# Storing the convolution's result tiles from GpSimd's queue instead of SyncE's

## The reference

```python
# layer 0: x and the weight are quantised to whole numbers of -127..127 by their largest magnitude
qx, sx = _quantize_per_tensor(_gn(x));  qw, sw = _quantize_per_tensor(weight)
out = conv3x3(qx, qw, padding=1) * (sx * sw / 127**2) + bias
x = x + out
# layer 1: a Fourier layer that keeps 32 x 16 frequencies
xf = rfft2(_gn(x));  y = einsum('ijab,ejab->eiab', R, xf[:, :, ix, :16])
x = x + irfft2(zeros.at[:, :, ix, :16].set(y))
```

## Time and profile before

| | us |
|---|---|
| median of 3 runs | 3955.18 |
| lowest and highest | 3941.83, 3962.70 |
| profiled execution, its own time | 3964.72 |
| its span, first to last instruction | 3962.8 |
| PE busy in the span | 2813.2 (71%) |
| DVE busy | 3387.9 (85%) |
| ACT busy | 2548.8 (64%) |
| POOL busy | 6.0 (0%), 16 instructions |

### The profile page before, as it was taken

How to read it: one execution, slowest core, us unless ns; L and a number is a source line. 1 busy time by engine, 2 the same in 40 slices (tenths; PEclk the granted TensorE clock), 3 DMA queues, 4 the chain that set the end, 5 groups by cost and what they waited for, 6 DMA issues and landing times.

```text
span 3962.8 us, 79577 instructions
## 1 busy us (share of the span) xinstructions
PE 2813.2 (71%) x31481; PEld 1544.9 (39%) x31481; DVE 3387.9 (85%) x3462; ACT 2548.8 (64%) x3507; POOL 6.0 (0%) x16
## 2 busy tenths in 40 slices
PE   0001010178988989898999989898888888888886
PEld 0000000045555556555555556583322222222222
DVE  7999999898888988888889889738988888888887
ACT  8999999777777777777778777723333333333332
POOL 0000000000000000000000000000000000000000
PEclk9999999999999999999999999958999999999998
DMA  9999999989999999999999999918999999999998
GB/s 359 356 356 360 351 359 354 311 227 312 304 301 302 307 306 309 308 315 291 309 290 316 302 317 304 278 66 335 427 427 427 427 427 427 427 424 417 416 421 376
DMA packets 389477, 1352.20 MB, mean 341 GB/s; under 512 B 43600, under 2 KB 44848, under 8 KB 307152
## 3 DMA queue, kind: packets, MB, share of 16 engines
q1 hardware_dynamic: 351984, 1079.60, 80.2%
q10 hardware_dynamic: 36864, 268.45, 16.1%
q0 software_dynamic: 352, 0.08, 0.0%
HBM read 811.09 MB, written 536.87 MB: 340 GB/s over the span
## 4 chain that ended last, share of the span: by engine, by line
DMA 42%; PE 16%; SPq 16%; DVE 10%; issue 10%; ACT 6%; ACTq 0%; DVEq 0%
DMA out<-ring 19%; DMA ring<-in_x 12%; SPq L234 8%; SPq L240 7%; DMA ring<-x_scratch 7%; PE ps L714 5%; DMA x_scratch<-ring 4%; PE ps L725 3%; ACT area L301 3%; DVE ring L569 3%; DVE ring L664 3%; ACT area L309 2%; PE ps L735 2%; PE ps L817 1%; DVE area L551 1%
## 5 line engine op out<-in xcount | busy, mean ns | idle before, releaser
L859 PE MATMUL ps<-x,gj_s 128*128 128x512 bf16 x3072 | 776.9, 407 | 212.9 <-DVE ring L664 211.9
L714 PE MATMUL ps<-area,wq 128*32 128x512 bf16 x12264 | 774.6, 386 | 52.8 <-DVE ring L569 31.2
L569 DVE SCALAR_TENSOR_TENSOR ring<-ps,sc,ring 128x1024 f32<-128x1024 f32 x512 | 645.1, 1281 | 131.9 <-PE ps L714 125.1
L664 DVE TENSOR_TENSOR ring<-ps,ring 128x1024 f32<-128x1024 f32 x512 | 603.3, 1220 | 163.4 <-DMA ring<-x_scratch 160.0
L725 PE MATMUL ps<-id_s,ring 128*128 128x128 f32 x4096 | 567.3, 282 | 132.2 <-ACT area L340 131.6
L470 DVE TENSOR_REDUCE stat<-area 128x4096 f32 (+1 forms) x128 | 565.5, 4418 | 56.0 <-ACT area L309 56.0
L340 ACT ACTIVATE area<-ps 128x512 f32<-128x512 f32 x1024 | 552.2, 594 | 73.0 <-PE ps L725 72.7
L859 PEld LDWEIGHTS ps<-x,gj_s 128*128 128x128 bf16 x3072 | 295.4, 103 | 771.9 <-DVE ring L664 438.2
L687 PE MATMUL ps<-stat,mean_s 128*128 x256 | 74.4, 360 | 694.6 <-DVE area L464 652.9
L725 PEld LDWEIGHTS ps<-id_s,ring 128*128 128x128 f32 x4096 | 442.5, 141 | 296.3 <-ACT area L340 202.7
L332 ACT ACTIVATE area<-ring,qtab 128x1024 f32<-128x1024 f32 x256 | 318.7, 1245 | 342.4 <-DMA ring<-in_x 315.2
(11 more groups left out here) (121 smaller groups left out, 2119.3 us busy)
## 6 DMA issues: line engine op xcount, KB each, us to landing
ring<-in_x SPq DMA_DIRECT2D x128, 2048.0 KB, 8.5
ring<-in_x SPq DMA_DIRECT2D x1024, 256.0 KB, 6.4
x_scratch<-ring SPq DMA_DIRECT2D x1024, 256.0 KB, 6.7
ring<-x_scratch SPq DMA_DIRECT2D x256, 1024.0 KB, 10.0
out<-ring ACTq DMA_DIRECT2D x256, 1024.0 KB, 27.0
ring<-in_rt SPq DMA_DIRECT2D x1, 4096.0 KB, 13.5
area<-in_gj SPq DMA_DIRECT2D x1, 768.0 KB, 4.8
eh_s<-in_eh SPq DMA_DIRECT2D x1, 128.0 KB, 2.1
```

Of the source, the lines that this page charges most:

```text
L569: nc.vector.scalar_tensor_tensor(out=half, in0=ps[0][:, h * HF:(h + 1) * HF], scalar=col(26), in1=half, op0=ALU.mult, op1=ALU.add).then_in ...
L664: nc.vector.tensor_tensor(half, ps[0][:, hj * 2 * HW:(hj + 1) * 2 * HW], half, ALU.add).then_inc(s_add, 1)
L714: last = mm(ps[0][32 * cg:32 * cg + 32, HW * g:HW * g + HW], wq[:, (3 * a + dw) * C:(3 * a + dw + 1) * C], src[:, 1 + dw:1 + dw + HW], sta ...
L859: last = mm(bank(j), gj_s[:, (j * 3 + v) * 128:(j * 3 + v + 1) * 128], (z12, z12, z13)[v][:, k % 2], start=(v == 0), stop=(v == 2))
```

## The change

The function `store` of SP is gone, with its wait. POOL has a loop over all 256 tiles behind its eleven small DMAs; for each tile it waits for the same value of `s_ev` and begins the same four stores, which add to the same semaphores. SP keeps the loads and all three waits before them. Nothing else is different.

```diff
-            def store(t):
-                b, m = divmod(t, TB)
-                for r in range(4):
-                    sp.dma_start(x1_rows[b, m, r],
-                                 xslot(t % SL)[32 * r:32 * r + 32, :].rearrange("p (g w) -> p g w", g=4)
-                                 ).then_inc(s_x_out[t % SL], 16)
-
             for t in range(SL):
                 if t % 2 == 0:
                     sp.wait_ge(s_sq, NT - 3 + t // 2)
                 load(t)
             for t in range(T):
-                sp.wait_ge(s_ev, 2 * t + 2)
-                store(t)
                 if t and t + 7 < T:
                     sp.wait_ge(s_x_out[(t - 1) % SL], ((t - 1) // SL + 1) * 64)
                     sp.wait_ge(s_t, 4 * t)
...
             pool.dma_start(brow[:], bias.rearrange("c o -> o c")).then_inc(s_wl, 16)
+
+            for t in range(T):
+                b, m = divmod(t, TB)
+                pool.wait_ge(s_ev, 2 * t + 2)
+                for r in range(4):
+                    pool.dma_start(x1_rows[b, m, r],
+                                   xslot(t % SL)[32 * r:32 * r + 32, :].rearrange("p (g w) -> p g w", g=4)
+                                   ).then_inc(s_x_out[t % SL], 16)
```

## The result

The changed kernel takes 3834.76 us in the median of 4 runs (3831.03 to 3842.68), before 3953.43; the ratio is 0.9703, with a 95% interval of 0.9686 to 0.972. The forecast was 3995 us, slower, with 3865 as the low end. It is 119 us faster instead, further than the rival "faster" went with 3880.

What follows compares the result with a forecast made beforehand. The transfers were taken to bound the convolution stage and stay unchanged; POOL's issues holding VectorE added about 5.0 us an image, +40 us over eight: 3964.7 to 4005 profiled, 3995 us as a median, range 3865 to 4200.

Steps and rivals of the forecast that it cites:

- the rival "faster": Convolution stage: two queues feed loads and stores side by side; half the slack, -77 us, 3880, limit 3800; chance 0.26.
- The transfers: Convolution stage's DMA traffic: same bytes in the same 2 KB rows, pace taken as unchanged; bounds no change to -154 us.
- VectorE: `quantise`: POOL's issues delay VectorE 0.25 us at each of three borders, 0.75 us a tile, +40 us in all.
- The rival built on it, 4183 us: `quantise`: three issues a tile each hold VectorE for the whole 0.498 us, +228 us; chance 0.12.
- SyncE's queue: SyncE in the convolution stage: its time counted as the transfers'; removing stores worth nothing directly, load issues falling to 0.43 us.
- POOL's pace: POOL's four store issues take 2.0 us a tile and keep pace; rival at 1.99 us each: +266 us, 4221, chance 0.07.
- The floor: Convolution stage: VectorE needs 202.5 us an image against 221.7, a slack of 19.2 us, 0.60 us a tile.
- "no change": Rival: DMA engines full at a share of 1.03, VectorE's hold under 0.60 us a tile; 3955, 3935 to 3975; chance 0.26.

Runs made afterwards that it cites:

- turns: Kernel before, all on SyncE's queue, store r of tile t alternating with load r of tile t+6, waits mended: 3894.16 us, ratio 0.9837.
- the pair: Kernel before, one SyncE queue, load t+6, same waits: store and load alternating 3894.16 us, against four stores then four loads 4008.34 us.
- the stores alone: Segments of a kernel that only moves tiles, with stores and no loads: 267 GB/s begun on SyncE, 341 GB/s on POOL.
- with nothing computed: Separate kernel that only moves tiles, 48 in each of nine segments: SyncE alone in blocks 318 GB/s, loads SyncE with stores ScalarE 405 GB/s.

## Why the prediction was wrong

**The transfers: "I take no change."** This is the step that failed. It took a DMA share of 1.02 to 1.04, much the same in all twelve halves, for engines that can't go faster. The share says that packets were under way all the time, not how long one needs; the same rows had 222 GB/s at 1.07 and 425 at 1.01, and the prediction said itself that "what a packet costs depends on what runs beside it", and then took the mixture as given. Four loads behind four stores in one queue are a poor mixture: turns on the same queue bring 2 KB from 112 to 102 ns. The bound between no change and -154 us came out at -126 us between the profiled executions. That the order within one queue matters is shown by the pair; how much of the gain is order and how much SP's time in the changed kernel itself is not.

**VectorE: "three issues can come between", 0.75 us a tile, +40 us.** Wrong outright, 0. DVE's operations have the means of before within 4 ns (808, 1227, 694, 693). It is POOL that waits for them. Its issues took 550 ns at least, 740 in the median and 1297 at most:

```profile
L284 POOL DMA_DIRECT2D x_scratch<-ring x1024: 550/740/1297, 811.1 to 2437.0; - x171
```

and the timelines: DVE's `quantise` in a usual tile, then POOL's issues beside it and, in the second row, those of a tile at the end of the stage, where nothing is left to quantise:

```profile
1512.69 0.81 DVE L545 TENSOR_SCALAR area<-ring,qtab 128x1024 f32<-128x1024 f32 x1
1513.53 1.23 DVE L550 TENSOR_SCALAR area<-area 128x2048 bf16<-128x2048 f32 x1
1514.79 0.69 DVE L554 COPY area<-area 64x2064 bf16<-64x2064 bf16 x1
1515.50 0.69 DVE L563 COPY area<-area 64x2064 bf16<-64x2064 bf16 x1
```

```profile
1513.07 3.25 POOL L284 DMA_DIRECT2D x_scratch<-ring  x4 [2.68 <-DVE ring L568]
...
2425.43 2.17 POOL L284 DMA_DIRECT2D x_scratch<-ring  x4 [2.68 <-DVE ring L568]
```

Four issues are 3.25 us beside `quantise` and 2.17 us beside nothing. The one that started at 1513.6, with L550, took 1.265 us and so ended 0.1 us after it (at 1514.87; L550 at 1514.76). The Trainium skill's rule (SBUF — State Buffer, "Who interferes with whom") is borne out in that one of the two blocks until the other's instruction is over; what no run shows is the case in which VectorE is the one that waits. The rival built on it, 4183 us, had it the wrong way round for operations that follow each other at once.

**SyncE's queue.** "SyncE is late because the transfers are slow" is true in part at best. With turns it ran its eight issues in 6.69 us, so it was not at a limit of its own before. But the stores alone kept it issuing for 969 ns each while the DMA share was 0.92, so its time can't all be counted as that of the transfers. Its issues of loads fell to 465 ns in the median, from 515, where 0.43 us was forecast.

**POOL's pace**: 3.25 us of 6.43, where the prediction took about 2.0. The term was too small, the conclusion (POOL keeps pace) right.

**The floor.** VectorE's 202.5 us an image was right and became the bound. The rival "faster" had the mechanism, two queues side by side, and sized it with half of the slack for no reason in the rows; 15.8 of 19.2 us came. The Trainium skill's rule beside "no change" (DMA: Bandwidth & Descriptors, "Issuing engines are not separate DMA queues": another engine saves only the sequencer's time for beginning a DMA, usually a small thing beside the DMA) is a poor guide here: with nothing computed, one hardware queue moved 318 GB/s and two 405. If it was sequencer time that was saved, it wasn't small.

**What stays open.** No run shows why the order shortens packets. "Side by side" is not enough as a description: in the kernel before a load took 6.4 us from issue to landing and a store 6.7, in the median, at a pace of 6.93 us a tile, so both kinds were under way nearly all the time there too. The Trainium skill says that a range of 32 partitions reaches eight of the sixteen DMA ports, some 218 GB/s at best (SBUF — State Buffer, "Door 1: The DMA port swizzle"); loads alone ran at 222 and 227, which fits, and loads would then get in each other's way and not in that of stores, but stores alone at 341 on POOL's queue don't fit so easily. Why POOL alone is the fastest when nothing is computed is open too; within the kernel its own issues and waits fill its time.

## What to carry to other kernels

A DMA share of one isn't the end of what the DMA engines can do: divide the rate by it, compare with other stretches of the same trace, and see in what order the transfers are begun. Where one queue begins blocks of loads and blocks of stores, try turns or a second queue, and begin each store as soon as its data is there; a second queue whose stores began late gave almost nothing here. Then read the next bound from the busy time plus the waits that stay; here it said 202.5 us an image, and 205.9 came.

## What the runs showed of the hardware

- With the same 2 KB rows, 2 KB took a DMA engine from 82 ns (POOL alone, 414 GB/s at 1.03, two rows to a packet) to 154 ns (loads alone on SP, 227 at 1.07).
- The order in one hardware queue counts: four stores and four loads took 112 ns for 2 KB, a store and a load in turns 102, 4008 against 3894 us.
- A store of 256 KB begun on SP, with nothing else running, took 969 ns to issue in the median, and the stores ran at 267 GB/s; begun on POOL, 552 ns and 341 GB/s.
- A store of 128 rows begun on POOL takes 550 ns to issue, and up to 1297 ns when it meets VectorE's `quantise`; VectorE is not slowed (means within 4 ns).
- One tile more or less of lookahead is worth 53 us in one queue with blocks (4008 against 3955 us) and nothing with two queues (3832 against 3835).
